# Output product as signs times a high and a low part, and residuals added to in PSUM, in a recurrent two-tower network on one core

## What is computed

```python
def _tower(x, w_in, b_in, blocks):
    h = _leaky(x @ w_in + b_in)
    for w1, b1, w2, b2 in blocks:
        h = _leaky(_leaky(h @ w1 + b1) @ w2 + b2 + h)
    return h
def step(prev_delta, xk):
    ...                                   # fk: 12 features, fk[:, 3] = prev_delta
    fe = _tower(fk[:, :4], fw_in, fb_in, flat_blocks)    # two blocks of 128x128
    pe = _tower(fk[:, 4:], pw_in, pb_in, path_blocks)    # two blocks of 128x128
    h = _leaky(concatenate([fe, pe]) @ cw1 + cb1)
    delta = sigmoid(h @ cw2 + cb2)[:, 0]
    return (delta, delta)
```

## Time and profile before

| | us |
|---|---|
| median of 3 runs | 1321.8 (1321.71 to 1322.02) |
| the profiled execution, its own time | 1322.16 |
| its span, first to last instruction | 1320.4 |
| PE busy | 1296.7 (98% of the span) |
| PE weight loads busy | 1071.2 (81%) |
| DVE busy | 853.9 (65%) |
| ACT busy | 828.5 (63%) |

### The profile page before, as it was taken

One profiled execution on the slowest core, in us unless ns is written; L12 is line 12 of the kernel. 1 busy time (PEld: TensorE's weight loads), 2 busy tenths in 40 slices (PEclk: granted clock), 3 DMA queues, 4 the chain that ended last, 5 costly groups with the idle time before them and its releaser, 6 DMA issues.

```text
span 1320.4 us, 18500 instructions
## 1 busy us (share of the span) xinstructions
PE 1296.7 (98%) x6016; PEld 1071.2 (81%) x6016; DVE 853.9 (65%) x1670; ACT 828.5 (63%) x1793; POOL 22.6 (2%) x19
## 2 busy tenths in 40 slices
PE   4999999999999999999999999999999999999998
PEld 2888888888888888888888888888888888888885
DVE  3666666666666666666666666666666666666665
ACT  2566666666666666666666666666666666666665
POOL 6000000000000000000000000000000000000000
PEclk9999999999999999999999999999999999999999
DMA  4400000000000000000000000000000000000000
GB/s 149 188 10 9 11 10 10 11 10 10 9 11 10 10 11 10 10 10 11 10 10 11 10 10 10 11 10 10 11 10 9 10 11 10 9 11 10 9 8 1
DMA packets 14022, 23.41 MB, mean 18 GB/s; under 512 B 6324, under 2 KB 6760, under 8 KB 13160
## 3 DMA queue, kind: packets, MB, share of 16 engines
q1 hardware_dynamic: 13640, 22.23, 5.7%
q10 hardware_dynamic: 288, 0.01, 0.0%
HBM read 15.66 MB, written 6.55 MB: 17 GB/s over the span
## 4 chain that ended last, share of the span: by engine, by line
PE 97%; DVE 1%; DMA 1%; ACT 0%; issue 0%; SPq 0%; ACTq 0%
PE ps_flat L394 34%; PE ps_path L394 34%; PE ps_head L479 8%; PE ps_head L484 8%; PE ps_head L490 8%; PE ps_path L406 2%; PE ps_flat L450 2%; DVE f_in L318 0%; DMA x_lo<-chunk_lo 0%; DVE f_t L351 0%; DMA chunk_x<-x 0%; DVE f_sum L321 0%; DVE p_sum L321 0%; DMA x_path<-x_lo 0%; ACT delta L277 0%
## 5 line engine op out<-in xcount | busy, mean ns | idle before, releaser
L229 ACT ACTIVATE f_mid<-ps_flat,columns_sb 128x256 f32<-128x256 f32 x512 | 242.4, 474 | 153.5 <-PE ps_flat L394 153.5
L394 PE MATMUL ps_path<-p_mid,hidden_w 128*128 128x256 f32 x1024 | 306.1, 381 | 0.8 <-ACT p_mid L229 0.8
L394 PE MATMUL ps_flat<-f_mid,hidden_w 128*128 128x256 f32 x1024 | 305.3, 380 | 0.0
L229 ACT ACTIVATE head<-ps_head,columns_sb 128x256 f32<-128x256 f32 x256 | 121.3, 474 | 246.0 <-PE ps_head L484 246.0
L394 PEld LDWEIGHTS ps_path<-p_mid,hidden_w 128*128 128x128 f32 x1024 | 195.9, 191 | 28.3 <-ACT p_mid L229 1.5
L394 PEld LDWEIGHTS ps_flat<-f_mid,hidden_w 128*128 128x128 f32 x1024 | 175.2, 189 | 46.2
L321 DVE SCALAR_TENSOR_TENSOR f_sum<-ps_flat,columns_sb,f_in 128x256 f32<-128x256 f32 x256 | 123.9, 484 | 129.1 <-PE ps_flat L394 129.1
L351 DVE SCALAR_TENSOR_TENSOR f_t<-delta,columns_sb,ps_flat 128x256 f32<-128x256 f32 x256 | 123.0, 480 | 98.3 <-ACT delta L277 93.3
L229 ACT ACTIVATE p_mid<-ps_path,columns_sb 128x512 f32<-128x512 f32 x256 | 174.8, 683 | 5.5 <-PE ps_path L394 5.5
L321 DVE SCALAR_TENSOR_TENSOR p_sum<-ps_path,columns_sb,p_in 128x512 f32<-128x512 f32 x128 | 96.1, 751 | 121.3 <-PE ps_path L394 121.3
L394 PE MATMUL ps_flat<-f_in,hidden_w 128*128 128x256 f32 x512 | 162.1, 398 | 5.1 <-DVE f_in L318 5.1
(11 more groups left out here) (32 smaller groups left out, 1266.6 us busy)
## 6 DMA issues: line engine op xcount, KB each, us to landing
x_path<-x_hi SPq DMA_DIRECT2D x256, 16.0 KB
x_path<-x_lo SPq DMA_DIRECT2D x256, 16.0 KB
x_flat<-x_hi SPq DMA_DIRECT2D x256, 6.0 KB
x_flat<-x_lo SPq DMA_DIRECT2D x256, 6.0 KB
chunk_x<-x SPq DMA_DIRECT2D x2, 1152.0 KB, 7.8
x_hi<-chunk_hi SPq DMA_DIRECT2D x2, 1152.0 KB, 9.3
x_lo<-chunk_lo SPq DMA_DIRECT2D x2, 1152.0 KB, 10.8
out<-delta SPq DMA_DIRECT2D x128, 2.0 KB
```

Source lines behind the costliest of these rows:

```text
L229: return act.activation(dst, src, ACT.Prelu, bias=bias, alpha=NEG)
L394: return pe.matmul(dst, weight[w_name], src, start=True, stop=True)
```

## The change

1. The output product. |cw2| is moved into the head: ACT computes leaky(|cw2| z + |cw2| cb1), with |cw2| as a per-partition scale operand and the scaled bias as the bias operand, and the product is with the signs of cw2 alone (fp32r). The head is written twice by ACT, as fp32 and as fp32r (head_high), DVE subtracts the two into an fp32r low part (head_low), and the product is two fp32r MATMULs of 256 columns, output_high and output_low, into one accumulation.
2. Residuals. In the flat tower DVE writes residual + bias to a new PSUM bank per group (ps_res; flat_1b_old, flat_2b_old), the second product of a block is added onto it, and ACT takes the leaky from PSUM for both blocks. The four DVE sums and DVE's flat_2b leaky go away. One product per group ahead of the loop opens the bank.
3. The path tower's first-block leaky (path_1b, 512 columns) moves from ACT to DVE.
4. The orders of the PE, ACT and DVE queues are written anew; flat_x waits for s_f2a_h in place of the second sum.

```diff
+        cw2_size, cb1_scaled, cw2_twice = sb("cw2_size", [HID, 1]), sb("cb1_scaled", [HID, 1]), sb("cw2_twice", [HID, 1])
+        cw2_sign = sb("cw2_sign", [HID, HID], fp32r)
...
# scalar
             def head_out(k, g):
                 if exists(k):
                     act.wait_ge(s_head_mm[g], k + 1)
-                    leaky(head[g][:, :], layer(ps_head, g), column["cb1"]).then_inc(s_head_h[g], 1)
+                    leaky(head[g][:, :], combined(g), cb1_scaled[:, :], cw2_size[:, :]).then_inc(s_head_h[g], 1)
+            def head_high(k, g):
+                if exists(k):
+                    act.wait_ge(s_head_mm[g], k + 1)
+                    leaky(head_hi[g][:, :], combined(g), cb1_scaled[:, :], cw2_size[:, :]).then_inc(s_head_hi[g], 1)
+            def flat_2b(k, g):
+                if exists(k):
+                    act.wait_ge(s_f2b_mm[g], k + 1)
+                    leaky(f_res2[g][:, :], layer(ps_res, g)).then_inc(s_f2b_h[g], 1)
...
             def body(k, par):
                 flat_1a(k, 0)
                 flat_1a(k, 1)
-                path_2a(k + 1)
                 flat_1b(k, 0)
                 flat_1b(k, 1)
                 flat_2a(k, 0)
                 flat_2a(k, 1)
+                flat_2b(k, 0)
+                path_in(k + 3)
+                flat_2b(k, 1)
                 head_out(k, 0)
-                path_in(k + 3)
+                head_high(k, 0)
                 head_out(k, 1)
+                head_high(k, 1)
                 delta_out(k, par, 0)
-                path_1b(k + 2, par)
+                path_1a(k + 3)
                 delta_out(k, par, 1)
-                path_1a(k + 3)
+                path_2a(k + 2)
# vector
+            def flat_1b_old(k, g):
+                if exists(k):
+                    dve.wait_ge(s_f_in_h[g], k + 1)
+                    if exists(k - 1):
+                        dve.wait_ge(s_f2b_h[g], k)
+                    else:
+                        dve.wait_ge(s_res_open[g], 1)
+                    dve.tensor_scalar(layer(ps_res, g), f_in[g][:, :], column["fr1_b2"], None,
+                                      ALU.add).then_inc(s_f1b_old[g], 1)
+            def head_low(k, g):
+                if exists(k):
+                    dve.wait_ge(s_head_h[g], k + 1)
+                    dve.wait_ge(s_head_hi[g], k + 1)
+                    dve.tensor_tensor(head_lo[g][:, :], head[g][:, :], head_hi[g][:, :].bitcast(fp32),
+                                      ALU.subtract).then_inc(s_head_lo[g], 1)
             def body(k, par):
                 flat_delta(k, par, 0)
                 flat_in(k, 0)
                 flat_delta(k, par, 1)
                 flat_in(k, 1)
-                path_2b(k, par)
-                flat_1b_sum(k, 0)
-                flat_1b_sum(k, 1)
+                flat_1b_old(k, 0)
+                flat_1b_old(k, 1)
+                flat_2b_old(k, 0)
                 path_1b_sum(k + 2)
-                flat_2b_sum(k, 0)
-                flat_2b(k, 0)
-                flat_2b_sum(k, 1)
-                flat_2b(k, 1)
+                flat_2b_old(k, 1)
+                path_1b(k + 2, par)
                 path_2b_sum(k + 1, 1 - par)
+                head_low(k, 0)
+                head_low(k, 1)
+                path_2b(k + 1, 1 - par)
# tensor: the new order of body(k, par), whole
+                flat_1a(k, 0)
+                combine_path(k, par, 1)
+                flat_1a(k, 1)
+                flat_1b(k, 0)
+                path_1b(k + 2, 1)
+                flat_1b(k, 1)
+                flat_2a(k, 0)
+                path_2b(k + 1, 0)
+                flat_2a(k, 1)
+                flat_2b(k, 0)
+                path_in(k + 3, 1 - par)
+                flat_2b(k, 1)
+                combine_flat(k, 0)
+                path_2b(k + 1, 1)
+                combine_flat(k, 1)
+                flat_x(k + 1, 1 - par, 1)
+                path_1a(k + 3, 0)
+                output_high(k, 0)
+                path_1a(k + 3, 1)
+                output_low(k, 0)
+                flat_x(k + 1, 1 - par, 0)
+                output_high(k, 1)
+                path_2a(k + 2, par, 0)
+                output_low(k, 1)
+                path_2a(k + 2, par, 1)
+                combine_path(k + 1, 1 - par, 0)
+                path_1b(k + 3, 0)
```

More of the change, by code:

```diff
@@ L77, in build @@
         ps_head = [bank(f"ps_head{g}") for g in range(GROUPS)]
+        ps_res = [bank(f"ps_res{g}") for g in range(GROUPS)]
         ps_path1, ps_path2 = bank("ps_path1"), bank("ps_path2")
@@ L226, in _, with leaky @@
             act.wait_ge(s_columns, 32)
-            def leaky(dst, src, bias=0.0):
-                return act.activation(dst, src, ACT.Prelu, bias=bias, alpha=NEG)
+            act.wait_ge(s_cw2, 1)
+            def leaky(dst, src, bias=0.0, scale=1.0):
+                return act.activation(dst, src, ACT.Prelu, bias=bias, scale=scale, alpha=NEG)
             def path_in(k):
@@ L394, in product, with onto @@
                 return pe.matmul(dst, weight[w_name], src, start=True, stop=True)
+            def onto(dst, w_name, src):
+                return pe.matmul(dst, weight[w_name], src, start=False, stop=True, skip_group_check=True)
             def filled(k, par):
@@ L460, in flat_1b @@
                     pe.wait_ge(s_f1a_h[g], k + 1)
-                    product(layer(ps_flat, g), "fr1_w2", f_mid1[g][:, :]).then_inc(s_f1b_mm[g], 1)
+                    pe.wait_ge(s_f1b_old[g], k + 1)
+                    onto(layer(ps_res, g), "fr1_w2", f_mid1[g][:, :]).then_inc(s_f1b_mm[g], 1)
             def flat_2a(k, g):
@@ L470, in flat_2b @@
                     pe.wait_ge(s_f2a_h[g], k + 1)
-                    product(layer(ps_flat, g), "fr2_w2", f_mid2[g][:, :]).then_inc(s_f2b_mm[g], 1)
+                    pe.wait_ge(s_f2b_old[g], k + 1)
+                    onto(layer(ps_res, g), "fr2_w2", f_mid2[g][:, :]).then_inc(s_f2b_mm[g], 1)
             def combine_path(k, par, g):
@@ L478, in combine_path @@
                         pe.wait_ge(s_delta[g], k)
-                    pe.matmul(layer(ps_head, g), weight["cw1_path"], cols(p_res2[par], g), start=True, stop=False)
+                    pe.matmul(combined(g), weight["cw1_path"], cols(p_res2[par], g), start=True, stop=False)
             def combine_flat(k, g):
@@ L483, in combine_flat, with output_high, output_low @@
                     pe.wait_ge(s_f2b_h[g], k + 1)
-                    pe.matmul(layer(ps_head, g), weight["cw1_flat"], f_res2[g][:, :], start=False, stop=True)\
+                    pe.matmul(combined(g), weight["cw1_flat"], f_res2[g][:, :], start=False, stop=True)\
                       .then_inc(s_head_mm[g], 1)
-            def output(k, g):
+            def output_high(k, g):
                 if exists(k):
                     pe.wait_ge(s_head_h[g], k + 1)
-                    pe.matmul(second(ps_head, g), cw2_rep[:, :], head[g][:, :], start=True, stop=True)\
+                    pe.wait_ge(s_head_hi[g], k + 1)
+                    pe.matmul(outcome(g), cw2_sign[:, :], head_hi[g][:, :], start=True, stop=False)
+            def output_low(k, g):
+                if exists(k):
+                    pe.wait_ge(s_head_lo[g], k + 1)
+                    pe.matmul(outcome(g), cw2_sign[:, :], head_lo[g][:, :], start=False, stop=True)\
                       .then_inc(s_out_mm[g], 1)
```

84 lines of the change are left out of this document (40 added, 44 removed).

## The result

The changed kernel takes 1307.8 us (median of 4 runs, 1307.29 to 1308.92) against 1321.8 for the kernel before (4 runs, 1321.33 to 1322.02): a ratio of 0.9896, 95% interval 0.9879 to 0.9913. The forecast was 1309 us, range 1286 to 1319.

The account below looks back on a forecast made before the run. TensorE's work was taken as the bound: 9.589 us plus stalls of 0.181 and 0.157 make a 9.927 us step, -13.9 us over 126 steps, with +1.0 at start-up: 1309 us, range 1286 to 1319.

Parts of the forecast that it names:

- What bounds the kernel: Whole step: TensorE's work is the bound, 9.987 of 10.037 us before; new work 9.589 us, 0.398 less.
- three signs of being wrong: TensorE waiting at flat_1b for the residual; flat_1a waiting for flat_in over 0.05 us; step under 9.8 at full scale-column price.
- the second stall: TensorE waits 0.157 us per step ahead of output_high(1) for group 1's head_high, behind four ACT head instructions.
- The residual: Flat tower: leaky from PSUM 0.38 us, DVE write to PSUM 0.45; about 0.5 us per block freed from the chain.
- The room of 0.56 for the first write: Group 0's flat_1b_old, between its earliest start and flat_1b(0), has 0.56 us, so a 0.45 us write is hidden.
- rival (c): Flat tower: residual writes are late; at 0.751 us a write, +0.19 us a step, 1333 us; chance 0.09.
- The first stall: TensorE waits 0.181 us per step ahead of flat_2b(1): 1.093 us stand where 1.274 are needed.
- Rival (a): The scale column on ACT's head instructions is free (0.474 us): step 9.770 us, 1289 us; chance 0.18.
- Small margins: Into the next step: flat_in(0) ends 0.20 and flat_in(1) 0.21 us before their flat_1a, where 0.17 is wanted; hidden.
- Start-up: Before step 0: VectorE's leakies and flat_ins around GpSimd's split cost 0 to +2.3 us, taken as +1.0.
- The sum: Whole run: step 9.927 us, 0.110 less, so -13.9 us over 126 steps, +1.0 at the start: 1309 us.

Follow-up runs that it names:

- the doubled write: The changed kernel with flat_1b's residual + bias written twice by VectorE, so that the write flat_1b waits for ends later: 1353.0 us.
- signs and parts in the old order: The kernel before with only the new output product (signs of cw2, high and low part), sums on VectorE and old orders kept: 1466.0 us.
- The pieces: GpSimd's splits of the later chunks issued in pieces of 384 columns: 1301.9 us on the changed kernel, 1317.3 us on the kernel before.

## Why the prediction was right

*What bounds the kernel.* TensorE's work plus its stalls. It holds: the work came out at about 9.58, for 9.589. That is 9.906 less 0.165, 0.136 and about 0.03 at output_high(0), where path_1a to path_1a take 0.57 for 0.55. The step was missed by 0.021, and starts printed to 0.01 us can't say which of these terms it belongs to. None of the three signs of being wrong came: TensorE waits neither at flat_1b for the residual nor for flat_in (1.1 us in all), and the step is not under 9.8. Taking the work back up (fp32 output) moved the step by +0.215: 0.398 of work less the second stall and what went with it, for head_high and head_low went too.

*The residual.* Priced at 0.38 and 0.45, measured 0.383 and 0.478 to 0.483. The room of 0.56 for the first write was too wide: flat_1b(0) wants the write's end 0.22 ahead, not 0.17, which makes it about 0.52. A write of 0.48 leaves 0.04, and the doubled write shows that from there all of it counts. So rival (c) was a real mechanism, held off by 0.04 us, and partly by luck, since the forecast's two errors (a link too short, a write priced 0.03 too low) both ate into the room. "It buys time only where the new PE order needs it" was too weak. With the sums back the same order loses 0.9 us a step, and signs and parts in the old order lose 1.1: in the orders that were run, the fp32r output is worth its 0.4 us only because the residuals take about 1.08 us out of the chain.

*The first stall.* 0.181 forecast, 0.165 measured. The leaky of f_mid2 is what it waits for; the link from product to product is 1.257 us (704.70 to 706.39 - 0.433) for 1.274.

*The second stall.* 0.157 forecast, 0.136 measured, plus the 0.03 at output_high(0). The scale column, which no row of before showed, costs 0.088 to 0.095 us. The page "ScalarE: Activation LUTs" of the Trainium skill, section "What ACT_TABLE_LOAD costs", has 93 ns for each pointer operand, and the trace agrees. Inside the term two errors cancelled: the pace of the four is 0.45, not 0.474, so the operand ends at 2.57 after combine_flat(0) (706.39 to 708.96) and not at 2.62; and output_high(1) goes at 709.30 - 0.117 = 709.18, 0.22 after its operand, not 0.17. Together they give the 2.79 of the forecast. The same 0.22 makes output_high(0), for which the forecast had no stall, wait its 0.03, and by so much TensorE is later at output_high(1). Rival (a) was the right price for a kernel without that operand: 9.770 and 1289 forecast, 9.745 and 1287.2 measured.

*Small margins.* flat_in(0) ends 0.21 and flat_in(1) 0.23 before their products, for 0.20 and 0.21.

*Start-up.* The term that was mis-sized: 1.0 more forecast, 2.17 measured, near the end (2.3) of its bounds. In that execution path_2b's leaky is held, all of step 0's VectorE work follows it, and TensorE is at the lower clock twice as long, for which the term had nothing. In the four runs where the first flat_in is held and the setup is unchanged, step 0's sigmoid is 1.0 to 1.4 us late, close to the forecast. The pieces show the mechanism: "SBUF — State Buffer", section "Who interferes with whom", of the Trainium skill has a DVE instruction with two SBUF inputs contend with a GpSimd instruction that reads SBUF, and in the traces it is held to about the end of the one instruction that runs: to 34.01 us in the changed kernel, whose subtraction ends at 33.46.

*The sum.* Steps 16.5 us less for 13.9, start-up 2.2 more for 1.0, the last step 0.1 more for nothing: the steps' miss of 2.6 us was half cancelled by start-up's of 1.2, so 1307.8 is nearer to 1309 than the terms deserve. No run undoes path_1b's move to VectorE by itself, so what it is worth isn't known.

## What to carry to other kernels

When the bound is one engine's queue in a recurrence, lay the new order out with start-to-start prices from the trace and look for every place where two dependent products stand closer than the link between them needs; each shortfall is paid once per step, and a scale or bias column of 0.09 us can be one. Put the link in at the price of its own kind: here a product goes 0.15 us after a leaky's end at flat_2b, but 0.22 after VectorE's write to PSUM or after head_high. A shorter chain and less work on the bound engine may each be worthless or harmful alone and pay together, so neither is judged by itself. A per-channel factor inside a loop belongs in the weights ahead of it, and a long background instruction that holds up another engine belongs in pieces.

## What was not expected of the hardware

Behind GpSimd's subtraction the cost is more than the hold: TensorE had 3.6 to 4.1 us without work, and its granted clock was 0.50 for 3.4 us in the kernel before and for 6.8 in the changed one. With pieces of 384 columns it stayed at 1.00, and the start came 6.9 us sooner in the changed kernel and 5.2 in the one before, where the longest held instruction took 4.76 us in each. Which instruction is held is not fixed by the program: with the same VectorE queue it was path_2b's leaky in two profiled executions (the changed kernel and f_mid2 without its bias) and the first flat_in in five. And a stall of 0.136 us per step, 17 us a run, has no row among the waits; it is seen in the starts alone.
